# Attention with relative positions and a feed-forward block on one core: the row maxima of both query halves are turned in one transpose

## The reference

```python
x = layernorm(x + attention(x))
x = layernorm(x + ffn(x))
```

## Time and profile before

| | |
|---|---|
| median of 3 runs | 2435.11 us (2433.6 to 2438.61) |
| profiled execution, its own time | 2437.13 us |
| its span | 2435.4 us |
| granted TensorE clock, mean | 0.975 |
| PE busy | 2263.2 us, 93% |
| DVE busy | 1746.0 us, 72% |
| ACT busy | 1670.8 us, 69% |
| POOL busy | 966.1 us, 40% |

### The profile page before, as it was taken

The page is one execution under the profiler, slowest core; times in us unless marked ns, Lnnn a source line. Parts: engine busy times, 40 slices in busy tenths (PEclk is TensorE's granted clock), DMA queues, the critical chain, the costliest instruction groups (busy, mean ns, idle before and its releaser), DMA issues. The chain is left out here.

```text
span 2435.4 us, 47764 instructions
## 1 busy us (share of the span) xinstructions
PE 2263.2 (93%) x14642; PEld 1272.1 (52%) x14642; DVE 1746.0 (72%) x3444; ACT 1670.8 (69%) x2239; POOL 966.1 (40%) x1565
## 2 busy tenths in 40 slices
PE   4998399999999999999999999999999999799997
PEld 3554144444444444444444444444444444688886
DVE  2454377777777777777777777777777773688885
ACT  2433157777777777777777777777777777466766
POOL 0000434444344443444334443444334432466663
PEclk9999579999999999999999999999999999899999
DMA  6998767777767777777777777777777762333311
GB/s 180 370 336 318 181 179 205 205 200 208 210 198 208 203 207 203 208 199 208 208 202 208 202 207 204 204 202 209 207 202 204 200 198 87 103 99 108 108 63 44
DMA packets 335292, 468.58 MB, mean 192 GB/s; under 512 B 90517, under 2 KB 263270, under 8 KB 335206
## 3 DMA queue, kind: packets, MB, share of 16 engines
q0 software_dynamic: 120960, 215.78, 35.0%
q1 hardware_dynamic: 201206, 243.05, 30.1%
q10 hardware_dynamic: 13040, 8.80, 1.2%
HBM read 244.73 MB, written 221.25 MB: 191 GB/s over the span
## 5 line engine op out<-in xcount | busy, mean ns | idle before, releaser
L896 ACT ACTIVATE probs<-weigh_ps 128x1024 f32<-128x1024 f32 x1024 | 1049.7, 1025 | 401.3 <-PE weigh_ps L1062 398.1
L1022 PE MATMUL ring_ps<-keys,queries 48*128 48x512 f32 x2048 | 839.3, 473 | 39.1 <-DVE partial_max L937 20.6
L948 DVE CUSTOM_DVE_ANT_1 ring_ps<-ring_ps,band_all 128x512 f32<-128x512 f32 x1008 | 681.0, 716 | 265.2 <-PE ring_ps L1022 265.0
L1062 PE MATMUL weigh_ps<-queries,keys 50*128 50x512 f32 (+3 forms) x2688 | 751.9, 385 | 1.4 <-ACT probs L896 0.8
L937 DVE TENSOR_REDUCE partial_max<-ring_ps 128x2 f32<-128x1024 f32 x512 | 627.9, 1226 | 165.7 <-PE ring_ps L1022 111.4
L1022 PEld LDWEIGHTS ring_ps<-keys,queries 48*128 48x128 f32 x2048 | 370.6, 187 | 517.9 <-issue 394.6
L1079 PE MATMUL sum_ps<-probs,values 128*32 128x512 f32 x4096 | 546.6, 605 | 0.1
L1047 PE MATMUL weigh_ps<-ident,band_all 128*128 128x128 f32 x2048 | 362.8, 290 | 22.8 <-ACT carried L884 20.2
L1062 PEld LDWEIGHTS weigh_ps<-queries,keys 50*128 50x128 f32 x2688 | 356.5, 186 | 17.7 <-ACT probs L896 9.5
L790 POOL DMA_DIRECT2D band_all<-band_scr x320 | 231.1, 725 | 332.9 <-DMA band_scr<-carried 318.3
L884 ACT ACTIVATE carried<-weigh_ps 128x512 f32<-128x512 f32 x512 | 302.6, 592 | 63.5 <-PE weigh_ps L1010 51.1
(11 more groups left out here) (115 smaller groups left out, 1858.6 us busy)
## 6 DMA issues: line engine op xcount, KB each, us to landing
band_scr<-carried SPq DMA_DIRECT2D x256, 512.0 KB, 4.0
band_all<-band_scr POOLq DMA_DIRECT2D x128, 512.0 KB, 6.6
band_all<-band_scr POOLq DMA_DIRECT2D x128, 256.0 KB, 3.3
keys<-k_scr POOLq DMA_DIRECT2D x128, 240.0 KB, 9.7
k_scr<-k_parts SPq DMA_DIRECT2D x16, 1792.0 KB, 8.4
q_scr<-q_parts SPq DMA_DIRECT2D x16, 1024.0 KB, 6.4
queries<-q_scr POOLq DMA_DIRECT2D x128, 128.0 KB, 2.9
o_scr<-weighted_s SPq DMA_DIRECT2D x64, 256.0 KB, 9.1
```

What stands on the lines that cost most here:

```text
L896: nc.scalar.activation(probs[:, u % PROBS], weigh_ps[weigh_of["scores", at]][:], ACT.Exp).then_inc(s_pr, 1)
L948: nc.vector.tensor_tensor_reduce(out=both, in0=both, in1=bias, scale=1.0, scalar=LOWEST, op0=ALU.add, op1=ALU.max, accum_out=partial_max[: ...
L1022: nc.tensor.matmul(dst, query_rows(c, h, ROWS, tile * P, (tile + 1) * P), key_rows(c, h, ROWS, c0, c0 + 512), start=True, stop=True, tile_ ...
L1062: last = nc.tensor.matmul(weigh_ps[weigh_of["scores", at]][:, h, e0 * P:e1 * P], key_rows(c, h, QROWS, k0, k0 + P), query_rows(c, h, QROWS ...
```

## The change

Both halves are kept in one tile each (`row_max`, `negative`, `negative_parts`), and POOL, PE, ACT and SP handle them once a step, at unit 10, as 16 instead of 8 numbers a partition, one transpose of 32 instead of 16 columns, one copy of 32 instead of 16 rows and one DMA a head of 16 instead of 8 pieces. At unit 4 nothing of this is left. With the turn gone there, the rule quoted above gives the look at unit 4 the heads in the order (1, 0) instead of (0, 1).

```diff
@@
-            row_max = sb("row_max", [P, 2, HG, QT], F32)
-            negative = sb("negative", [P, 2, HG, QT], F32)
-            negative_parts = sb("negative_parts", [P, 2, HG, PARTS, QT], F32)
-            zero = sb("zero", [P, HG, QT], F32)
-            minus_max = sb("minus_max", [HG * PARTS * QT, 2, P], F32R)
+            row_max = sb("row_max", [P, HG, 2, QT], F32)
+            negative = sb("negative", [P, HG, 2, QT], F32)
+            negative_parts = sb("negative_parts", [P, HG, PARTS, 2, QT], F32)
+            zero = sb("zero", [P, HG, 2, QT], F32)
+            minus_max = sb("minus_max", [HG * PARTS * NT, P], F32R)
...
-            TURN_AT = {4: 0, 10: 1}
+            TURN_AT = 10
 
             def turns_at(step, u):
-                return u in TURN_AT and 0 <= step + 1 < G
+                return u == TURN_AT and 0 <= step + 1 < G
...
             def turn_index(step, u):
-                return 2 * (step + 1) + TURN_AT[u]
+                return step + 1
...
-                def load_minus_max(i, step, g):
+                def load_minus_max(i, step):
                     c = step + 1
-                    sp.wait_ge(s_tc, cnt(i, 2, 2 * c + g + 1))
+                    sp.wait_ge(s_tc, cnt(i, 1, c + 1))
                     for h in range(HG):
                         r0 = h * ROW_TILE + ROWS
-                        rows = queries[r0:r0 + PARTS, c % SLOTS, g * 512:(g + 1) * 512].bitcast(F32)
-                        sp.dma_start(rows.rearrange("r (a p) -> r a p", a=QT),
-                                     minus_max[h * PARTS * QT:(h + 1) * PARTS * QT, g, :].bitcast(F32)
-                                     .rearrange("r (a p) -> r a p", a=1)).then_inc(s_min[g][c % SLOTS], 16)
+                        rows = queries[r0:r0 + PARTS, c % SLOTS, :].bitcast(F32)
+                        sp.dma_start(rows.rearrange("r (a p) -> r a p", a=NT),
+                                     minus_max[h * PARTS * NT:(h + 1) * PARTS * NT, :].bitcast(F32)
+                                     .rearrange("r (a p) -> r a p", a=1)).then_inc(s_min[c % SLOTS], 16)
...
-                def minus_maxima(i, step, g):
+                def minus_maxima(i, step):
                     c = step + 1
-                    done = cnt(i, 2, 2 * c + g + 1)
-                    pool.wait_ge(s_rm, done)
-                    nc.gpsimd.tensor_tensor(negative[:, g], zero[:], row_max[:, g], ALU.subtract)
...
+                    pool.wait_ge(s_rm, cnt(i, 2, 2 * c + 2))
+                    nc.gpsimd.tensor_tensor(negative[:], zero[:], row_max[:], ALU.subtract)
...
@@ step_of, on POOL
-                    if 0 <= step + 1 < G:
-                        minus_maxima(i, step, 0)
                     read_chunk(i, step, 0)
...
                     read_chunk(i, step, 1)
                     if 0 <= step + 1 < G:
-                        minus_maxima(i, step, 1)
+                        minus_maxima(i, step)
...
-                    nc.vector.tensor_reduce(row_max[:, g], partial_max[:, g], AX_X, ALU.max).then_inc(s_rm, 1)
+                    nc.vector.tensor_reduce(row_max[:, :, g], partial_max[:, g], AX_X, ALU.max).then_inc(s_rm, 1)
...
                 def turn_max(i, n):
-                    g = n % 2
-                    pe.wait_ge(s_mm, cnt(i, 2, n + 1))
+                    pe.wait_ge(s_mm, cnt(i, 1, n + 1))
                     dst = ring_bank(i, ("turn", n))
-                    nc.tensor.transpose(dst[0:HG * PARTS * QT, 0:P],
-                                        negative_parts[:, g].rearrange("p h c t -> p (h c t)"),
+                    nc.tensor.transpose(dst[0:HG * PARTS * NT, 0:P],
+                                        negative_parts[:].rearrange("p h c g t -> p (h c g t)"),
                                         ident[:]).then_inc(s_turn, 1)
...
                     if u < 2:
-                        pe.wait_ge(s_min[g][c % SLOTS], i * (16 * HG) + 16 * HG * (c // SLOTS + 1))
+                        pe.wait_ge(s_min[c % SLOTS], i * (16 * HG) + 16 * HG * (c // SLOTS + 1))
```

More of the change, by code:

```diff
@@ L607, in post_ln_block @@
             s_tc = sem("minus_max_copied")
-            s_min = [[sem(f"minus_max_in{g}_{a}") for a in range(SLOTS)] for g in range(2)]
+            s_min = [sem(f"minus_max_in{a}") for a in range(SLOTS)]
             s_sc = sem("scores_ready")
@@ L740, in unit @@
                     if turns_at(step, u):
-                        load_minus_max(i, step, TURN_AT[u])
+                        load_minus_max(i, step)
                     if u == 5 and step > 0:
@@ L805, in read_bands @@
                                      ).then_inc(s_b[m], 16)
-                def minus_maxima(i, step, g):
+                def minus_maxima(i, step):
                     c = step + 1
-                    done = cnt(i, 2, 2 * c + g + 1)
-                    pool.wait_ge(s_rm, done)
-                    nc.gpsimd.tensor_tensor(negative[:, g], zero[:], row_max[:, g], ALU.subtract)
-                    nc.gpsimd.tensor_tensor(negative_parts[:, g, :, 0].bitcast(F32R), zero[:], row_max[:, g],
+                    pool.wait_ge(s_rm, cnt(i, 2, 2 * c + 2))
+                    nc.gpsimd.tensor_tensor(negative[:], zero[:], row_max[:], ALU.subtract)
+                    nc.gpsimd.tensor_tensor(negative_parts[:, :, 0].bitcast(F32R), zero[:], row_max[:],
                                             ALU.subtract).then_inc(s_neg, 1)
-                    pool.wait_ge(s_neg, done)
-                    nc.gpsimd.tensor_tensor(negative_parts[:, g, :, 1], negative[:, g], negative_parts[:, g, :, 0],
+                    pool.wait_ge(s_neg, cnt(i, 1, c + 1))
+                    nc.gpsimd.tensor_tensor(negative_parts[:, :, 1], negative[:], negative_parts[:, :, 0],
                                             ALU.subtract).then_inc(s_mm, 1)
@@ L887, in copy_turned @@
                 def copy_turned(i, n):
-                    act.wait_ge(s_turn, cnt(i, 2, n + 1))
-                    nc.scalar.activation(minus_max[:, n % 2, :], ring_ps[0:HG * PARTS * QT, slot_of["turn", n], 0:P],
+                    act.wait_ge(s_turn, cnt(i, 1, n + 1))
+                    nc.scalar.activation(minus_max[:], ring_ps[0:HG * PARTS * NT, slot_of["turn", n], 0:P],
                                          ACT.Copy).then_inc(s_tc, 1)
@@ L986, in wait_for @@
                         elif kind == "turn":
-                            pe.wait_ge(s_tc, cnt(i, 2, n + 1))
+                            pe.wait_ge(s_tc, cnt(i, 1, n + 1))
                         elif kind == "scores":
```

## The result

| | before | after |
|---|---|---|
| median of 15 runs each | 2438.26 us | 2425.77 us |
| lowest and highest | 2433.6, 2443.22 | 2423.21, 2435.83 |
| ratio (95% interval) | | 0.9954 (0.9943 to 0.9965) |
| span of the profiled execution | 2435.4 us | 2423.6 us |
| median step (eight pairs) | 27.42 us | 27.29 us |

The change makes the kernel faster by 0.46%, 11.2 us of 2438.3. The forecast was 2.5 us less. The measured time lies inside the range, but at the end that the first rival held: each step gives 0.12 us and not 0.02.

What follows compares the result with a forecast made beforehand. PE was taken to set the pace, but to wait for ACT's band copy at unit 4 and POOL at unit 10. 1.2 + 0.8 + 0.4 + 0.1 = 2.5 us less than 2435.11 gives 2432.6 us; range 2424 to 2438.5 us.

Steps and rivals of the forecast that it cites:

- first rival: Unit 4: the exponential doesn't hold PE, so the second look's 0.16 us a step stays gained; 11.1 us, 2424 us; chance 0.12.
- the prediction's own sign: Forecast wrong if a step shrinks by more than 0.08 us, or unit 10's look starts later than 0.11 us behind DVE's end.
- both readings: PE sets the pace mid-attention; at the change's two places it waits for ACT's band copy (20.2 us) and POOL's subtraction (23.7 us).
- Unit 4, steps 1 to 61: Removed turn becomes wait for ACT's band copy; 0.02 us a step gained, 1.2 us in all, ends 0 and 9.8 us.
- Step -1: Removed turn of unit 4 where no scores are made: a pair takes 2.87 instead of 3.64 us, 0.8 us gained.
- Steps 0 and 62: Removed turn of unit 4 in the first and last of these steps: 0.4 us and 0.1 us gained.
- Unit 10: Remaining turn, 62 steps: POOL's subtractions and PE's weight load lengthen the chain by 0.09 us, inside the cover; cost 0.
- The cover: Unit 10, turn to first look: PE ready after 0.70 of 0.82 us, as the look waits for DVE; 0.12 us spare.
- the second rival: Unit 10: POOL's subtractions outgrow the cover, 0.18 us a step, 11 us slower before gains, 2444 us; chance 0.09.
- What else moves: Fewer POOL subtractions, ACT copy, SP DMAs and waits, half 0's maxima travelling with half 1's: each 0.

Runs made afterwards that it cites:

- bare turn: Changed kernel with one PE transpose of 16 identity columns left at unit 4, neither copied nor read; ratio to the kernel before 0.9956, step 27.29 us.
- copied turn: Changed kernel with a spare transpose at unit 4 that ACT copies, second look waiting for it, heads (0, 1); ratio to the kernel before 0.9994, step 27.42 us.
- old order: Changed kernel with the heads of unit 4 in the order (0, 1), no turn or copy there; ratio to the kernel before 0.9946, step 27.29 us.
- two turns in the band's bank: Kernel before with both turns (units 4 and 10) in the bank of the band product; ratio to the kernel before 1.0009, step 27.37 us.
- one turn in the band's bank: Changed kernel with unit 10's turn in unused columns of the band product's bank, copied behind the band; 2417.68 us, ratio to the kernel before 0.9925.

## Why the prediction was right, and where it was not

**The time and the range.** The time lies in the range because the range took in the first rival, whose reason doesn't hold; for the forecast that is luck. By the prediction's own sign the forecast is wrong: a step was to shrink by no more than 0.08 us, and shrank by 0.12.

**What bounds the kernel.** Right in both readings: behind the turn of unit 4 stands ACT's band copy, and the turn's time became wait (20.2 to 32.8 us; the bare turn shows it from the other side). The wait grew by 0.21 us a step, not by the whole 0.28: the row after shows 0.61 us idle, where 0.7 was forecast.

**Unit 4, steps 1 to 61: the term that was mis-sized.** The prediction took 0.02 us a step, "as the seventh pair shows", counted "from the transposes to that point", where that point was the first look behind the exponential. All numbers to there came true to 0.01 us. The measure ended too early. Two chains leave the second look: PE's own order (band product, weighted sums, the next unit's first look), where the wait for the exponential takes most of the delay in, and which is what was followed; and DVE's reduction, which waits for that look and frees the ring bank of unit 5's second look. The second chain reaches PE 0.35 us behind the end of the count. Measured in place of 1.2 us: 61 x 0.125 = 7.6 us. That the copy started this delay is shown by two runs (with the copy 27.42, without it 27.29, each with the transpose). That it runs by the reduction and bank 0 is read from the timelines: with the copy (before, copied turn) the second look of unit 5 starts 0.05 us behind the end of the reduction in the median step, and its weight load with it; without the copy (after, bare turn, old order) it is 0.16 us, and the load is 105 ns ahead. No run moved that link by itself.

**The first rival** gave 2424 us, near the 2425.77 measured, but for a reason that doesn't hold: it had the exponential not binding. It binds, and 0.13 us are given back there.

**Other steps.** Step -1: 0.76 us measured, 0.8 forecast. Steps 0 and 62 with what else isn't a middle step: 8.4 - 7.6 = 0.8 us measured, 0.5 forecast.

**Unit 10.** Cost 0, right. The growth was sized too high: 15 ns a subtraction (24 forecast), 7 ns a weight load (21). The cover is larger than the 0.12 us that was read. So the second rival fell twice. The Trainium skill says in "Perfetto Trace Analysis" (Optimizing Scalar/DVE Operations) that smaller pieces may let work be done sooner where ScalarE or VectorE isn't saturated but causes bubbles on another engine; the prediction carried this over to POOL, of which the sentence doesn't speak. It found no case here: the usual bubble at POOL's subtraction had next to no price (one more subtraction: nothing in the median step; unit 12, without the bubble: 0.06 us a step).

**What else moves.** At no cost, right: the saved work of POOL, SP and the DMAs had no effect (the copied turn). That half 0's maxima meet their date at unit 10 is right, and unit 14 shows that four units later they don't.

**What stays open.** The ratio says 11.2 us, the attention accounts for 9.2. Behind the last weighted sums the profiles of the two kernels before show 366.1 and 365.9 us, of the changed one 362.9 and 364.3; the other kernels with one turn at unit 10 in the ring 363.1 to 364.4, the copied turn 367.6, two turns in the band's bank 368.0, but one there 365.9. With the one turn at unit 12 it is 366.6, in the kernel before with its second turn there 367.8. So about 2 us may belong to the kernel and not to chance, but one turn less doesn't bring them by itself, and nothing that was run tells what does.

## What to carry to other kernels

When an instruction is removed, follow every chain that leaves what it delayed, and count to the point where the two cases meet again on the bounding engine, not to the next wait that looks binding; a comparable place without the instruction, read one pair further, gave 0.12 us where 0.02 was taken. A wait in the profile is a price only if nothing else holds the same engine just behind it: 26 us of short waits for POOL went with the turn's move to unit 12, and that gave 0.06 us a step, about 4 us. And the same small transpose was free in front of a wait, cost 0.12 us by the bank it occupied, and 0.27 us where it stood behind the wait.

## What the runs showed of the hardware

A look that just has to wait for its bank loses more than it comes late. The second look of unit 5 starts only 0.03 us later before than after, but the next instruction of PE follows it 0.10 us later, and its weight load starts with it where it starts 0.11 us ahead otherwise.

A step of its own kind stands in the second run of the kernel before: PE took 30.57 us for it where its neighbours took 27.4. POOL's band load ahead of the three subtractions waited for the DMA of a band to land, and the subtractions stand behind this load in POOL's order:

```profile
424.86 0.78 POOL L803 DMA_DIRECT2D band_all<-band_scr  x1 [8.04 <-DMA band_scr<-carried]
```

In the same step of the first run this load is issued at 419.15; counted from the first weighted sums (328.7 and 332.3 us), it is 2.1 us later in the second. So PE stood idle ahead of the turn of unit 10, for 1.73 us, where the same row has no idle time:

```profile
426.35 0.28 PE L1030 MATMUL ring_ps<-ident,negative_parts 128*16 128x128 f32 x1 [1.73 <-POOL negative_parts L815]
```

Right behind that wait the granted clock was 0.50, which is 1.2 GHz:

```profile
427.10:430.50 3.40, 3.40 (x16) 1.21 (x18) 1.23 (x1) 1.51 (x2) 1.65 (x3) 0.50 0.43 150
```

The pair with the wait took 1.9 us more than usual, the next one 1.0 us more. One such step costs 3.2 us, a quarter of the whole change, so the median step is the better measure for a change of 0.1 us a step. The profiles of the bare turn and the copied turn have one such step each (waits of 1.3 and 1.9 us), the one with one turn in the band's bank has one (1.5 us), and the one with one more subtraction has three (1.4, 2.8 and 2.6 us); its profiled execution, 2435.53 us, is the longest of its nine. In all of them the same load of POOL was late, and in all but the one of 1.4 us the clock was at 1.2 GHz from 0 to 1.5 us behind the end of the wait. The profiles with the turn at unit 12 have no such step. So POOL's chain does have a price at unit 10, not in the usual step but in a rare one. Why the band is written late at times, and whether one more subtraction makes it more frequent, stays open.

In the run with the turn at unit 14, where PE waits for the maxima 1.44 us a step on average, the clock fell in 42 of the steps, each time within 1.7 us behind the end of the wait, and stayed at 1.00 in the others. These steps were 1.9 us longer than the others.
